# Two-stage graph and expert kernel: second layer two steps behind the first, a fifth row slot, and fills between the row scatters

## What is computed

```python
x = x + gnn(layernorm(x))            # adj @ h and adj.T @ h, three sigmoid gates, relu
# ffn(h): 8 experts, two of them for each token
gate_logits = xf @ Wg + bg
top_w, top_i = jax.lax.top_k(gate_logits, 2);  top_w = softmax(top_w)
for e in range(E):
    h = gelu(xf @ W1[e] + b1[e])     # 128 -> 512
    out = out + w_dense[:, e:e+1] * (h @ W2[e] + b2[e])   # 512 -> 128
x = x + ffn(layernorm(x))
```

## Time and profile before

| | us |
|---|---|
| median of 3 runs (769.83 to 773.42) | 772.68 |
| the profiled execution's own time | 766.71 |
| its span | 764.9 |
| its mean granted TensorE clock | 0.913 of 2.4 GHz |

### The profile page before, as it was taken

One profiled execution on the slowest core, in us unless ns is written; L12 is line 12 of the kernel. 1 busy time (PEld: TensorE's weight loads), 2 busy tenths in 40 slices (PEclk: granted clock), 3 DMA queues, 4 the chain that ended last, 5 costly groups with the idle time before them and its releaser, 6 DMA issues.

```text
span 764.9 us, 18892 instructions
## 1 busy us (share of the span) xinstructions
PE 689.8 (90%) x5004; PEld 627.9 (82%) x5004; DVE 625.5 (82%) x2129; ACT 515.6 (67%) x1389; POOL 501.9 (66%) x460
## 2 busy tenths in 40 slices
PE   3879999799997549999998999999999999999991
PEld 2557677577675439999998999998999999999990
DVE  5989986889989648888888788887888888888881
ACT  3888878478875326676776677776677777777770
POOL 1534656365665774655678578886888888888883
PEclk9997977578887559999999999999999999999996
DMA  8465878463522266578857867459764543544310
GB/s 255 145 203 159 287 261 97 80 140 106 208 92 76 98 189 187 180 216 285 254 169 242 258 176 192 129 173 359 225 170 127 140 126 99 152 124 126 86 43 15
DMA packets 100336, 127.07 MB, mean 166 GB/s; under 512 B 37367, under 2 KB 61824, under 8 KB 100240
## 3 DMA queue, kind: packets, MB, share of 16 engines
q1 hardware_dynamic: 81600, 83.41, 39.4%
q0 software_dynamic: 17344, 42.51, 16.6%
q10 hardware_dynamic: 1296, 0.14, 0.2%
HBM read 71.41 MB, written 56.99 MB: 168 GB/s over the span
## 4 chain that ended last, share of the span: by engine, by line
PE 50%; DMA 4%; issue 1%; POOL 1%; SPq 0%; POOLq 0%; DVE 0%
PE bank L1262 7%; PE bank L1264 7%; PE bank L1263 7%; PE bank L1276 7%; PE bank L1277 7%; PE bank L1281 7%; DMA w_t<-w_split 4%; PE bank L1290 3%; PE bank L1252 3%; POOL out_dram L645 1%; SPq L482 0%; POOLq L151 0%; SPq L466 0%; DVE row L1137 0%; SPq L476 0%
## 5 line engine op out<-in xcount | busy, mean ns | idle before, releaser
L767 ACT ACTIVATE act_f<-bank,b_t 128x256 f32<-128x256 f32 x560 | 220.0, 476 | 42.6 <-PE bank L1264 41.8
L645 POOL DMA_INDIRECT out_dram<-row,to_row x140 | 182.0, 1300 | 47.6 <-issue 36.3
L648 POOL DMA_INDIRECT rows<-row,to_row x140 | 162.5, 1160 | 76.5 <-DVE row L1137 46.7
L610 POOL DMA_INDIRECT rows<-row,slot_low x128 | 131.3, 1026 | 93.2 <-DVE row L833 58.1
L1125 DVE TENSOR_TENSOR act_lo<-act_f,act_hi 128x1024 fp32r<-128x1024 f32 x140 | 170.3, 1216 | 0.1
L1262 PE MATMUL bank<-in_hi,w_t 128*128 128x256 f32 x560 | 158.1, 282 | 4.0 <-DMA w_t<-w_split 4.0
L1264 PE MATMUL bank<-in_hi,w_t 128*128 128x256 f32 x560 | 157.3, 281 | 0.0
L1263 PE MATMUL bank<-in_lo,w_t 128*128 128x256 f32 x560 | 156.8, 280 | 0.0
L1276 PE MATMUL bank<-act_hi,w_t 128*128 128x256 f32 x560 | 149.6, 301 | 1.5 <-DMA w_t<-w_split 1.3
L1277 PE MATMUL bank<-act_hi,w_t 128*128 128x256 f32 x560 | 137.5, 280 | 0.0
L775 ACT ACTIVATE y_t<-bank,b_t 128x256 f32<-128x256 f32 x140 | 66.7, 476 | 99.8 <-PE bank L1281 99.8
(11 more groups left out here) (173 smaller groups left out, 1239.3 us busy)
## 6 DMA issues: line engine op xcount, KB each, us to landing
row<-rows SPq DMA_DIRECT2D x140, 260.0 KB, 2.9
w_t<-w_split SPq DMA_DIRECT2D x40, 512.0 KB, 5.2
xs<-in_x_dram SPq DMA_DIRECT2D x16, 512.0 KB, 4.4
rows<-ends_rep SPq DMA_DIRECT2D x14, 260.0 KB, 5.1
b_t<-biases SPq DMA_DIRECT2D x140, 2.5 KB
rows<-row,to_row POOLq DMA_INDIRECT x140
out_dram<-row,to_row POOLq DMA_INDIRECT x140
row<-in_L_ffn_W_dram SPq DMA_DIRECT2D x4, 512.0 KB, 9.7
```

Of the source, the lines that this page charges most:

```text
L610: pool.indirect_dma_start(out=rows, out_offset=bass.IndirectOffsetOnAxis(ap=slot_low[:, r, b:b + 1], axis=0), in_=row[:, r, b, :], in_offs ...
L645: pool.indirect_dma_start(out=out_rows, out_offset=at, in_=got[:, g, j, P:2 * P], in_offset=None, bounds_check=TOKENS - 1, oob_is_err=Fals ...
L648: pool.indirect_dma_start(out=rows, out_offset=at, in_=got[:, g, j, :], in_offset=None, bounds_check=NROWS - 1, oob_is_err=False).then_inc ...
L767: last = act.activation(act_f[:, s, c, :], ps_h[s][:, c, :], ACT.Gelu, bias=b_t[:, w, c:c + 1])
```

## The change

- Experts: layer 2 of unit k-2 (not k-1) stands in PE's step k, the output transposes of unit k-5 (not k-2), and the transposes of the rows of unit k+3 (not k+2) come last in the step (before: ahead of layer 2). Buffers grow accordingly: `in_hi` and `in_lo` 3, `act_hi` and `act_lo` 3, `y_t` 5. PSUM banks are given out anew, one half of a hidden layer at a time. The steps are written out in full instead of looped, and each pass is filled and drained by itself. The four SP calls for a unit keep their order, and rows are still asked for 4 units ahead.
- Graphs: `row` and `slot_low` have five slots. Between the 8 scatters of a chunk GpSimd fills a tile of 256 columns with zeros and waits for the fill (7 per chunk, 112 in all). The last four chunks signal on semaphores of their own (`s_late`, counted in order by `s_land`). All bias copies move up, behind the expert weight loads (b2 behind the stores of four low parts).
- Second pass: the table of what a unit needs is used for 12 units instead of 8.

```diff
-    EARLY = 2 * AHEAD
+    EARLY = [2 * AHEAD, 3 * AHEAD]
+    IN, BACK = 3, 5
+    LATE = 2
+    RING = 5
...
-        row = sb("row", [P, 4, G, ROW])
+        row = sb("row", [P, RING, G, ROW])
...
+        pause = sb("pause", [P, 2 * P])
...
             for k in range(4, E):
                 load_w(k)
+            biases(0, E)
...
-            load_x(chunk_of(10))
-            biases(0, E // 2)
-            load_x(chunk_of(11))
-            biases(E // 2, E)
...
                 def ready(k):
-                    if k % AHEAD == 0:
-                        sp.wait_ge(s_row[k // AHEAD], 16 * G * CHUNKS // 4)
-                    for i in range(k // AHEAD + 1, 4):
-                        sp.wait_ge(s_row[i], least[k] & 1023)
+                    if k == AHEAD:
+                        sp.wait_ge(s_land, 2)
+                    sp.wait_ge(s_land, least[k] & 7)
...
                     for b in range(G):
                         pool.indirect_dma_start(out=rows, out_offset=bass.IndirectOffsetOnAxis(ap=slot_low[:, r, b:b + 1], axis=0),
                                                 in_=row[:, r, b, :], in_offset=None, bounds_check=NROWS - 1,
-                                                oob_is_err=False).then_inc(s_row[r], 16)
+                                                oob_is_err=False).then_inc(landing, 16)
+
+                        if b < G - 1:
+                            own(pool.memset(pause[:], 0.0))
+                            own.sync()
...
-            for k in range(CHUNKS):
+            for k in range(CHUNKS + 1):
                 scatter_rows(Turn(k // UA, k % UA, UA, CHUNKS))
+                if k > PART:
+                    pool.wait_ge(s_late[k - 1 - PART], 16 * G)
+                    pool.sem_inc(s_land, 1)
...
-                    wait_slot(dve, s_row, 16 * G, two, 0)
+                    left = two.index - RING
+                    if left >= 0:
+                        dve.wait_ge(s_row[left % 4], 16 * G * (left // 4 + 1))
...
+            for p in range(PASSES):
+                units = of_pass(p)
+                for k in units[:IN]:
+                    unit_turned(unit(k))
+                for k in units:
+                    layer1(unit(k))
+                    if k - BACK in units:
+                        unit_back(unit(k - BACK))
+                    if k - LATE in units:
+                        layer2(unit(k - LATE))
+                    if k + IN in units:
+                        unit_turned(unit(k + IN))
+                for k in units[-BACK:-LATE]:
+                    unit_back(unit(k))
+                for k in units[-LATE:]:
+                    layer2(unit(k))
+                for k in units[-LATE:]:
+                    unit_back(unit(k))
```

More of the change, by code:

```diff
@@ L65, in wait_slot @@
     wait_turn(eng, sems[s], each, Turn(turn.group, (turn.step - s) // ring, turn.unroll // ring, 0), more)
[L68 to L91, removed]
 class Own:
@@ L864, in turn @@
                 if one.real:
-                    sums(0, one, xs, G // 2)
-                    last = sums(0, one, xs, G // 2 + 2)
+                    sums(0, xs[:, one.slot(4)], G // 2)
+                    last = sums(0, xs[:, one.slot(4)], G // 2 + 2)
                     if not two.real:
@@ L871, in turn @@
                     for b in range(0, G, 2):
-                        last = sums(1, two, row[:, :, :, P:2 * P], b)
+                        last = sums(1, row[:, two.index % RING, :, P:2 * P], b)
                     summed = own(last)
@@ L1061, in _ @@
             own.sync()
-            first, rows_of, seg, lim, at, start = (unit[:, i] for i in range(6))
+            first, rows_of, seg, lim, at, start = (unit_at_[:, i] for i in range(6))
             own(dve.scalar_tensor_tensor(out=change[:], in0=expert[:, 2], scalar=1.0, in1=expert[:, 0], op0=ALU.max, op1=ALU.not_equal))
@@ L1141, in step @@
-            def step(t, second):
-                sum_up(t.back(2), second)
-                hidden_hi(t)
-                tile_lo(t.on(2))
-                hidden_lo(t)
-            for k in range(2):
-                tile_lo(unit_at(k))
-            k = turns(dve, UT, UNITS, lambda t: step(t, 0), UNIT_SPANS[:1])
-            for k in range(k, UNIT_SPANS[1][0] * UT):
-                step(unit_at(k), int(k - 2 >= NU))
-            with dve.Fori(*UNIT_SPANS[1]) as g:
-                for s in range(UT):
-                    step(Turn(g, s, UT, UNITS), 1)
@@ new lines, in _ @@
+            for p in range(PASSES):
+                units = of_pass(p)
+                for k in units[:IN - 1]:
+                    tile_lo(unit(k))
+                for k in units:
+                    if k - BACK - 1 in units:
+                        sum_up(unit(k - BACK - 1))
+                    if k + IN - 1 in units:
+                        tile_lo(unit(k + IN - 1))
+                    hidden_hi(unit(k))
+                    hidden_lo(unit(k))
+                for k in units[-BACK - 1:]:
+                    sum_up(unit(k))
@@ new lines, in unit_turned @@
+                if t.index - IN in units:
+                    wait_turn(pe, s_done, 1, t, -IN - BACK if t.index - IN - BACK > units[0] else units[0] - t.index)
+                elif units[0] > 0:
+                    outputs = [k for k in range(units[0]) if bank_of_outputs(k) == bank_of_rows(t.index)]
+                    pe.wait_ge(s_done, outputs[-1] + 1)
+                for j in range(BLK):
+                    last = pe.transpose(ps_x(t)[:, j * P:(j + 1) * P], got[:, g, j, 0:P], ident[:])
@@ new lines, in unit_back @@
+            def unit_back(t):
+                wait_turn(pe, s_y, 1, t, 1)
+                if t.index + BACK + 1 in of_pass(t.index // NU):
+                    wait_turn(pe, s_inlo, 1, t.on(BACK + 1), 1)
+                else:
+                    wait_turn(pe, s_done, 1, t, -2)
+                for j in range(BLK):
+                    last = pe.transpose(ps_o(t)[:, j, :], y_t[:, t.slot(BACK), j * P:(j + 1) * P], ident[:])
+                last.then_inc(s_o, 1)
+            pe.wait_ge(s_slot, CHUNKS)
```

289 lines of the change are left out of this document (135 added, 154 removed).

## The result

| | before | changed |
|---|---|---|
| median, us | 771.25 (4 runs, 768.44 to 773.42) | 862.60 (4 runs, 861.59 to 864.25) |
| profiled execution's own time, us | 766.71 | 861.59 |
| its span, us | 764.9 | 859.5 |
| its mean granted TensorE clock | 0.913 | 0.878 |

The changed kernel is slower: ratio 1.119, 95% interval 1.114 to 1.123. The forecast was 833 us with a range up to 846. So the sign was right, and the time lies 29 us above the forecast and outside the range.

A forecast was written before the change was run, and what follows sets the result against it. PE was taken to bound the experts, DVE and PE to be nearly full in the graphs, where GpSimd would then set the pace. Terms 36.4 + 3.7 + 17 + 3 + 6 = +66 on 766.7 gave 833 us, range 765 to 846.

The forecast's parts named there:

- The pause: Graphs, GpSimd: each fill and its wait between scatters costs 0.82 us, 0.32 fill plus 0.50 of exposed scatter start.
- A chunk of 16.0 us: Graphs: a chunk's scatters on GpSimd grow from 10.3 to 16.0 us, so GpSimd sets the pace; unit 7 comes +36.4 us.
- The bias copies: Graphs, SP's queue: moved to the first turns, costed at nothing; up to 4 us lost if they last into chunk 4's load.
- The fifth slot: Graphs: removes DVE's waits for a slot of `row`, 12 us taken, but swallowed by GpSimd's slower pace.
- From the last scatter to unit 7: Start of experts: 3.1 us until unit 7's rows are asked for, then 3.9 for them to land; PE transposes at 336.
- Changes of expert: Experts: at 9 changes PE waits for rows queued behind second-layer weights (16 us) and late first-layer loads (7); +17 with bounds.
- Between the passes: Experts: PE waits for gelu, the last two outputs and the split of the first new unit, together +3 us.
- Order and last units: Experts: +3.7 us for work PE has left when unit 7 is transposed, +6 for the last scatters, ending 13 behind PE.
- the cheap fill: Rival, graphs: scatter start is prepared during the fill, a pause costs 0.35 to 0.5 us; 789 to 796 us; chance 0.25.
- The faster case: Rival: fills are hidden, the fifth slot brings experts 15 us earlier, rows and weights land in time; 759 us; chance 0.14.
- fills slow DVE: Rival, graphs: each fill holds DVE for 0.32 us, 31 us over 14 turns; 820 us; chance 0.05.
- the forecast case: Whole kernel: a pause of 0.6 to 1.1 us, GpSimd pacing the graphs; own range 805 to 865 us; chance 0.48.

The follow-up runs named there:

- e12: Changed kernel with fills of 4 columns instead of 256, GpSimd still waiting for each: 839.5 us, ratio 1.089.
- e13: Changed kernel with 256-column fills into seven tiles in turn, no scatter waiting for the fill just before it: 805.9 us, ratio 1.050.
- e2: Changed kernel, fills kept, with the bias copies back behind the loads of chunks 10 and 11: 854.4 us, ratio 1.109.
- e3: Changed kernel without fills and with the bias copies back behind the loads of chunks 10 and 11: 802.9 us, ratio 1.039.
- e4: Kernel before the change, with only the fills and their waits added between a chunk's 8 scatters: 828.0 us, ratio 1.074.
- e14: Changed kernel, fills included, with the load of x for chunk 4 ahead of the eight bias copies: 863.4 us, ratio 1.118.
- e1: Changed kernel without the 112 fills and the waits for them, all else as changed: 801.9 us, ratio 1.042.
- e7: Experts of the kernel before behind the graphs of e3 (five slots, no fills): 763.8 us, ratio 0.991.

## Why the forecast was right in kind and 29 us short

The pause and the waits at the changes of expert, its two main mechanisms, came as forecast. What failed is that two costs stood in the sum at nothing: the bias copies, up to 8.3 us, and TensorE's clock behind new idle time, about 12.7 (3.7 at the restart, some 9 at the changes). A third term was sized too small, the chunk on GpSimd, 8.6 us. One of the first two alone would not have brought the time of the profiled execution, 861.6, under the range's end of 846; both would. Term by term:

- **The pause**: right, 0.82 us taken, 0.82 measured; e12 and e13 show that the start of the next scatter behind the wait is the larger part of it, as the forecast derived from a scatter behind DVE.
- **A chunk of 16.0 us**: 16.5 measured, (345.90 - 81.29) / 16. The scatters took 1.03 us in the mean, not 0.98, though the first and the last row already had 1.16 and 1.33: the duration of one row was carried over 128, 6.3 us. The rest are stray gaps, one of 2.6 us among them. Together 8.6 us over 16 chunks.
- **The bias copies**: the step that failed first. "I cost them at nothing", with 4 us as the bound, because only loads of x stand behind them; but such a load was due. DVE waited 8.4 us for chunk 4, the first scatter came 8.3 us later than in the profile before, and in a stage that GpSimd now paced, none of it was hidden. Against the starts of 74.7 to 75.7 in e2, e3 and e4 it is 5.6 to 6.6 us. No place near it is free either: e2 gained 8.2 us, e14, one load later, nothing.
- **The fifth slot**: 12 us taken, 10.7 in e1's turns. It was rightly left out of the sum, as GpSimd paced the graphs. (The count scan at 240.02, called the last in the forecast, is the thirteenth of 16; nothing hangs on it.)
- **From the last scatter to unit 7**: 7.0 us forecast, 350.46 - 345.90 = 4.6 measured, 2.4 less. With the chunk and the copies this makes the 14.5 us by which unit 7 is later than forecast.
- **Restart**: the second step that failed, missing from the sum. After 25 us idle PE worked at 0.69 of its clock, +3.7 us. From unit 7 to unit 10 `in_lo` takes 13.4 us here, and 10.2 in e1 and in e3, which have the same experts and no such idle time ahead of them.
- **Changes of expert**: the waits were forecast well, +17. PE's waits behind unit 7 for rows (14.0) and weights (10.0), less 5.5 before, are 18.5. What was missing is the clock during and behind them: 0.84 over 42 us in the second pass, some 7 us, and 0.91 from 480 to 500, some 2 (an estimate, length times the missing share). It agrees with the table: 13.0 + 17.9, less the 3.6 between the passes, is 27.3, and 18.5 of it are waits. That these idle spells themselves lower the clock is an argument from the rows; no run isolates it.
- **Between the passes**: +3 forecast, 3.6 idle measured.
- **Order and last units**: 3.7 + 6 = 9.7 forecast, 9.1 measured. The last scatter ends 11.5 us behind PE, not 13.
- **The plain step**: 3.25 us forecast and measured.

Of the rivals, the cheap fill falls by the 0.80 in the trace and by e1. The faster case falls with it, and by e3: even without fills the new order of the experts costs more than the fifth slot gives. That fills slow DVE is not borne out: the median of the 16 slot sums is 1.224 us in the changed kernel and 1.225 before, and twelve turns take 162.9 us in e13, with all its fills, and 162.4 in e1 without any. The rule of the Trainium skill (SBUF — State Buffer, the section on the two separate sides), by which fills that read nothing leave such operations alone, agrees. The range was too narrow on the slow side. It ended at 846, though the forecast case's own range went to 865, and that bound stood for dearer pauses, not for a term costed at nothing, nor for the clock: that 861.6 lies under 865 is chance.

## What to carry to other kernels

Before adding a wait on an engine's own work, look at what the next instruction hides behind the one before it: here a scatter's start was hidden in a row and open behind any wait, and 112 such waits cost 57 us (e13 against the changed kernel), more than everything else in the change. In a queue served in order, a load that waits for a later release delays all that stands behind it, so a consumer that is moved back by a step moves the whole queue; when such a deeper order is planned, ask first which release feeds the head of the queue. And cost a transfer that is moved at the moment of the load that stands next behind it, not by how idle the engines are.

## What the runs showed that I had not expected

- Copies of a few KB in elements of 4 bytes are expensive in every place tried: 8.4 us of DVE wait ahead of chunk 4, 9.8 ahead of chunk 5, 4.7 behind the last load, and beside the last scatters 14.5 us for 2 KB and 24.4 us for 4 KB, with a median of 6.6 us for the scatters' landing. Behind chunks 10 and 11, with five slots and no fills, they cost no slot wait, but in e7 6.8 us of wait for x.
- Issuing one load of x took 0.4 us on SP's queue in most places, 10.06 us behind the copies and four stores (e14).
- GpSimd starts a scatter 0.17 us behind a fill that it need not wait for, 0.30 behind another scatter, 0.80 behind a fill that it waits for, be it 0.12 or 0.33 us long, and 0.80 behind DVE.
- The same kernel took 871.7 us on one chip and 769 to 772 on the others; what differs there was not looked into.
